# Issuing the weight casts at the start of the program instead of behind the attention strips

## The chip, the cores and the metric

The kernel runs as one program on all 8 NeuronCores of one Trainium2 chip. Each core has its own engines (TensorE, VectorE, ScalarE, GpSimd or POOL, and SyncE, which here only issues DMAs) and 16 DMA engines, and each gets its own copy of the inputs. No core waits for another. The metric is the device time in microseconds (us) of the slowest core.

## The reference

One layer: a layernorm, then an attention-like block with sigmoid scores, a mixture of 8 experts (top 2) plus a shared expert, and the residual. `x` is (2, 8192, 1024).

```python
xn = _layernorm(x, axis=-1)
# attention: C, R = 16, 64; SCALE = 0.03125
qz_u = xn @ ternary_factor_u.T * SCALE          # split into 16 channels of 64
qz_v = xn @ ternary_factor_v.T * SCALE
qh = sigmoid(einsum('bcsr,bctr->bcst', qz_u, qz_v))
qh_v1 = einsum('bcst,bctr->bcsr', qh, qz_v)
qh_v2 = einsum('bcst,bcsr->bctr', qh, qz_u)
message_G = (qh_v1 @ ternary_factor_u + qh_v2 @ ternary_factor_v) * SCALE
# experts: E, H = 8, 2048
w_full = softmax over the top 2 of (xn @ Wr) * SCALE, spread over E
h = einsum('bsd,edh->bseh', xn, W1) * silu(einsum('bsd,edh->bseh', xn, W3))
out = einsum('bsed,bse->bsd', einsum('bseh,ehd->bsed', h, W2), w_full)
out = out + ((xn @ Ws1) * silu(xn @ Ws3)) @ Ws2
return x + message_G + out
```

All inputs are float32. The kernel multiplies in bfloat16.

## The kernel before

A core takes one batch element and owns 2048 of its 8192 rows; it computes `u` and `v` projections for all 8192 rows and everything else for its own. There are four stages.

**Front** (from L383). `ut`, `vt` and `wr` are loaded by 17 DMAs of POOL, which cast float32 to bfloat16 on the way (L393 to L399, semaphore `s_w`); the token of the last is `wprep_tok`. Then 64 tiles of 128 rows are loaded by SyncE (L461, three buffers `xb`), normalized (statistics in `emit_tile_front` at L466 and L469, normalization at L510 in `emit_tile_back`) and transposed (L519). After every fourth tile `emit_group_projs` multiplies the group of 512 rows (L545 feature-major, L573 token-major) and SyncE stores the results to DRAM: `zu_fm` and `zv_fm` (L558), `zu_tm` and `zv_tm` (L587), and for the first four groups `xnT_hb` (L594) beside the router. The loop emits `emit_tile_front(j)` ahead of `emit_tile_back(j - 1)`, so tile 4's load and statistics stand ahead of group 0's projections, and tile 5's load stands behind all stores of group 0 in SyncE's order.

**Strips** (`strip`, L704 to L761). For 16 channels, twice, SyncE loads slices of the stored projections, TensorE computes scores (L724), ScalarE the sigmoid (L750), TensorE the second product (L743). The first waits of this stage are `fence_a = sch.fence()`, which holds the present count of every semaphore.

**Output projection** (L807, L811). 16 DMAs load `ub` and `vb`, the bfloat16 copies of the factors; they wait for `precast_tok`.

**Experts** (`emit_ffn_phase`, L182 to L280). SyncE loads slices of the bfloat16 weights `w1b`, `w3b`, `w2b`, `ws1b`, `ws3b`, `ws2b` from DRAM, which also wait for `precast_tok`; then the residual is added and the result stored.

The bfloat16 copies of the weights are made in DRAM by 29 DMAs of POOL that read float32 and write bfloat16 (L773, L778), 27 of 4 MB written and 2 of 2 MB. Everything is put into per-engine lists by `Sched`; each engine runs its list in order. `Sched.finalize` adds one kind of wait: a DMA that raises a semaphore first waits for the highest count at or below the semaphore's count so far that anyone waits for. So loads and stores of one semaphore are largely issued one behind the landing of another.

Of the kernel before, what the change touches and what calls it, by code (L numbers as in the profile page):

```python
# [20 lines left out]
E = 8  # L21
# [268 lines left out]
def build_nc(debug_stage=4):  # L290
# [5 lines left out]
    u_in = nc.dram_tensor("u_in", [D, D], F32, kind="ExternalInput").ap()  # L296
    v_in = nc.dram_tensor("v_in", [D, D], F32, kind="ExternalInput").ap()
    wr = nc.dram_tensor("wr", [D, E], F32, kind="ExternalInput").ap()
    rb_rep = nc.dram_tensor("rb_rep", [128, E], F32, kind="ExternalInput").ap()
    w1 = nc.dram_tensor("w1", [E, D, H], F32, kind="ExternalInput").ap()  # L300
    w2 = nc.dram_tensor("w2", [E, H, D], F32, kind="ExternalInput").ap()
    w3 = nc.dram_tensor("w3", [E, D, H], F32, kind="ExternalInput").ap()
    ws1 = nc.dram_tensor("ws1", [D, H], F32, kind="ExternalInput").ap()
    ws2 = nc.dram_tensor("ws2", [H, D], F32, kind="ExternalInput").ap()
    ws3 = nc.dram_tensor("ws3", [D, H], F32, kind="ExternalInput").ap()

    out = nc.dram_tensor("out", [OWN, D], F32, kind="ExternalOutput").ap()
# [6 lines left out]
    w1b = nc.dram_tensor("w1b", [E, D, H], BF16, kind="Internal").ap()  # L314
    w2b = nc.dram_tensor("w2b", [E, H, D], BF16, kind="Internal").ap()
    w3b = nc.dram_tensor("w3b", [E, D, H], BF16, kind="Internal").ap()
    ws1b = nc.dram_tensor("ws1b", [D, H], BF16, kind="Internal").ap()
    ws2b = nc.dram_tensor("ws2b", [H, D], BF16, kind="Internal").ap()
    ws3b = nc.dram_tensor("ws3b", [D, H], BF16, kind="Internal").ap()
    ub = nc.dram_tensor("ub", [D, D], BF16, kind="Internal").ap()  # L320
    vb = nc.dram_tensor("vb", [D, D], BF16, kind="Internal").ap()
# [32 lines left out]
    with ExitStack() as ctx:  # L354
# [4 lines left out]
        s_ld = en(nc.semaphore("s_ld"))  # L359
        s_st = en(nc.semaphore("s_st"))  # L360
        s_w = en(nc.semaphore("s_w"))
        sch = Sched([s_t, s_v, s_s, s_ld, s_st, s_w])
# [29 lines left out]
        for dc in range(8):  # L392
            sch.emit("gpsimd", lambda e, dc=dc: e.dma_start(  # L393
                out=ut_sb[:, dc * 1024:(dc + 1) * 1024], in_=ut[dc * 128:(dc + 1) * 128, :]),
                inc=s_w, inc_k=16)
            sch.emit("gpsimd", lambda e, dc=dc: e.dma_start(
                out=vt_sb[:, dc * 1024:(dc + 1) * 1024], in_=vt[dc * 128:(dc + 1) * 128, :]),
                inc=s_w, inc_k=16)
        sch.emit("gpsimd", lambda e: e.dma_start(  # L399
            out=wr_sb, in_=wr.rearrange("(dc p) e -> p dc e", p=128)), inc=s_w, inc_k=16)  # L400
        wprep_tok = sch.tok(s_w)

        if debug_stage == 5:
            sch.emit("sync", lambda e: e.dma_start(
                out=xnT_hb[:, :], in_=tb["xnT_in"][:, :]), inc=s_st, inc_k=16)
            sch.emit("sync", lambda e: e.dma_start(out=wT_sb, in_=tb["wT_in"][:, :]),
                     inc=s_ld, inc_k=16)
# [3 lines left out]
                w1b=w1b, w2b=w2b, w3b=w3b, ws1b=ws1b, ws2b=ws2b, ws3b=ws3b,  # L411
                precast_tok=precast_tok))
            fence = sch.fence()
            sch.emit("sync", lambda e: e.dma_start(out=tb["acc_out"][:, :], in_=acc),
                     waits=fence, inc=s_st, inc_k=16)
# [247 lines left out]
        for j in range(OWN_T):  # L663
            t_tok = sch.emit("tensor", lambda e, j=j: e.transpose(
                a2_ps[0:8, 0:128], wfull_sb[:, j * 8:(j + 1) * 8], idf_sb),
                waits=[wf_tok] + list(tr_free[0]), inc=s_t)
            ev = sch.emit("vector", lambda e, j=j: e.tensor_copy(
                wT_sb[0:8, j * 128:(j + 1) * 128], a2_ps[0:8, 0:128]),
                waits=[t_tok], inc=s_v)
# [96 lines left out]
            strip(zv_fm, zv_tm, zu_fm, qh1_sb)  # L766
            strip(zu_fm, zu_tm, zv_fm, qh2_sb)

        a_done_tok = sch.tok(s_ld)
        first_pc = [True]  # L770
        for ei_ in range(E):
            for (dst_, src_) in ((w1b, w1), (w2b, w2), (w3b, w3)):
                sch.emit("gpsimd", lambda e, dst_=dst_, src_=src_, ei_=ei_: e.dma_start(  # L773
                    out=dst_[ei_], in_=src_[ei_]),
                    waits=([a_done_tok] if first_pc[0] else []), inc=s_w, inc_k=16)
                first_pc[0] = False
        for (dst_, src_) in ((ws1b, ws1), (ws2b, ws2), (ws3b, ws3), (ub, u_in), (vb, v_in)):
            sch.emit("gpsimd", lambda e, dst_=dst_, src_=src_: e.dma_start(  # L778
                out=dst_[:, :], in_=src_[:, :]), inc=s_w, inc_k=16)
        precast_tok = sch.tok(s_w)  # L780


        if debug_stage >= 3:
            fence_s = sch.fence()
            ab.reset_to(32768)
# [2 lines left out]
            for fc in range(8):  # L788
                sch.emit("sync", lambda e, fc=fc: e.dma_start(
                    out=u_sb[:, fc * 1024:(fc + 1) * 1024], in_=ub[fc * 128:(fc + 1) * 128, :]),  # L790
                    waits=fence_s + [precast_tok], inc=s_ld, inc_k=16)
                sch.emit("sync", lambda e, fc=fc: e.dma_start(
                    out=v_sb[:, fc * 1024:(fc + 1) * 1024], in_=vb[fc * 128:(fc + 1) * 128, :]),
                    waits=fence_s + [precast_tok], inc=s_ld, inc_k=16)
# [5 lines left out]
            for dc in range(8):  # L800
                for sg in range(4):
                    pi = gi % 2

                    def do_g(e, dc=dc, sg=sg, pi=pi):
# [13 lines left out]
                        waits=[mm], inc=s_v)  # L818
# [3 lines left out]
        if debug_stage >= 4:  # L822
            emit_ffn_phase(nc, sch, (s_t, s_v, s_s, s_ld, s_st, s_w), ab, af, ps, dict(
                acc=acc, sel_sb=sel_sb, wT_sb=wT_sb, xnT_hb=xnT_hb, const_tok=const_tok,
                w1b=w1b, w2b=w2b, w3b=w3b, ws1b=ws1b, ws2b=ws2b, ws3b=ws3b,
                precast_tok=precast_tok))
# [10 lines left out]
            for j in (range(OWN_T) if RESID else ()):  # L837
                sl = j % 2
                x_tok = sch.emit("sync", lambda e, j=j, sl=sl: e.dma_start(
                    out=xb2[sl], in_=xf[j * 128:(j + 1) * 128, :]),  # L840
                    waits=xb2_free[sl], inc=s_ld, inc_k=16)

                def do_trr(e, j=j):
# [9 lines left out]
                    waits=[tr_tok, x_tok] + ob_free[sl], inc=s_v)  # L853
# [3 lines left out]
                    out=out[j * 128:(j + 1) * 128, :], in_=ob[sl]),  # L857
                    waits=[o_tok], inc=s_st, inc_k=16)
                ob_free[sl] = [st_tok]

        if debug_stage < 4:
            fence = sch.fence()
            pairs = [("zu_fm", zu_fm), ("zv_fm", zv_fm), ("zu_tm", zu_tm), ("xnT", xnT_hb)]
            for (k, src) in pairs:
                sch.emit("sync", lambda e, k=k, src=src: e.dma_start(out=dbg[k][:, :], in_=src[:, :]),
                         waits=fence, inc=s_st, inc_k=16)
            sch.emit("sync", lambda e: e.dma_start(out=dbg["wfull"][:, :], in_=wfull_sb),
                     waits=fence, inc=s_st, inc_k=16)
            if debug_stage >= 2:
                sch.emit("sync", lambda e: e.dma_start(out=dbg["qh1"][:, :], in_=qh1_sb),  # L870
                         waits=fence, inc=s_st, inc_k=16)
                sch.emit("sync", lambda e: e.dma_start(out=dbg["qh2"][:, :], in_=qh2_sb),
                         waits=fence, inc=s_st, inc_k=16)
            if debug_stage >= 3:
                sch.emit("sync", lambda e: e.dma_start(out=dbg["acc"][:, :], in_=acc),
                         waits=fence, inc=s_st, inc_k=16)
# [55 lines left out]
```

How the kernel before makes its waits and increments, by code:

```python
        def op(e, fn=fn, wl=tuple(wl), inc=inc, inc_k=inc_k, prewait=prewait):  # L80
            if prewait[0] is not None:
                e.wait_ge(*prewait[0])
            for (s, v) in wl:
                e.wait_ge(s, v)
            r = fn(e) if fn is not None else None
            if inc is not None and r != "self_inc":
                if r is None:
                    r = e.nop()
                r.then_inc(inc, inc_k)
# [107 lines left out]
                def ld13(e, wsl=wsl, h0=h0, srcs=srcs):  # L197
                    o3 = w13[wsl].rearrange("p (dc x) -> p dc x", dc=8)
                    e.dma_start(out=o3[:, :, 0:256],
                                in_=srcs[0].rearrange("(dc p) h -> p dc h", p=128)[:, :, h0:h0 + 256]).then_inc(s_ld, 16)
                    e.dma_start(out=o3[:, :, 256:512],
                                in_=srcs[1].rearrange("(dc p) h -> p dc h", p=128)[:, :, h0:h0 + 256]).then_inc(s_ld, 16)
                    return "self_inc"
```

## Time and profile before

| what | us |
|---|---|
| median of 2 runs | 11241.76 |
| the two runs | 11203.61, 11279.91 |
| profiled execution, as timed | 11147.0 |
| span of its slowest core (core 7) | 11145.1 |
| spans of its cores | 10733.6 to 11145.1 |

In the profile, L12 is line 12 of the kernel. The engines are PE (TensorE matmuls), PEld (TensorE weight loads), DVE (VectorE), ACT (ScalarE), POOL and SP (SyncE); a `q` behind an engine is its instruction queue, which issues DMAs. L82 and L84 are the waits that `Sched` emits. DMA queue q1 carries what SyncE issues, q0 what POOL issues; a packet in the queue rows is one contiguous piece that one DMA engine moves, or the small write that raises the semaphore at the end. A share is of the 16 DMA engines' time. `arena_b` and `arena_f` are the bfloat16 and float32 buffers in SBUF, and `ps` is PSUM. PEclk is TensorE's granted clock as a share of 2.4 GHz.

### The profile page before, as it was taken

Reading aid. Unit: us, or ns where it says so; the run is one execution under the profiler, and the core shown is the slowest. Engines: PE = TensorE matmul, PEld = TensorE weight load, DVE = VectorE, ACT = ScalarE, POOL = GpSimd, SP = SyncE. Lnnn points to the kernel's source line nnn. Section 1 sums busy time; section 2 is a strip of 40 time slices with the busy share of each in tenths; the row PEclk is TensorE's granted clock in tenths of the full one; section 3 lists DMA queues with packets and bytes.
Section 4 is the critical chain, followed back from the end, with each engine's and each line's share of the span. In section 5 each row is a group of like instructions: output and inputs, shape, how many; then the busy total and the mean of one; then the engine's idle time right before and its main releaser. Section 6 shows DMA issues by size and latency. Waiting matters only on the chain.

```text
span 11145.1 us, 93354 instructions; the slowest of 8 cores (10733.6 to 11145.1 us)
## 1 busy us (share of the span) xinstructions
PE 9510.1 (85%) x35632; PEld 2981.4 (27%) x35632; DVE 1290.9 (12%) x2145; ACT 4734.7 (42%) x4795; POOL 24.5 (0%) x50
## 2 busy tenths in 40 slices
PE   5667789999999999999999996003899999999997
PEld 2233321112222121122221121001344444444443
DVE  3333310000000000000000000000222222222222
ACT  1111137668998795599985696000000010100000
POOL 0000000000000000000000000000000000000000
PEclk8788867669998795599995698556999999999998
DMA  3222210000000000000000039996333333333333
GB/s 82 72 68 72 72 46 17 9 9 18 18 18 18 9 18 14 13 18 18 18 18 9 9 42 110 110 111 81 97 98 89 102 87 98 91 96 97 91 102 117
DMA packets 726796, 635.32 MB, mean 57 GB/s; under 512 B 279256, under 2 KB 611160, under 8 KB 720736
## 3 DMA queue, kind: packets, MB, share of 16 engines
q1 hardware_dynamic: 718976, 507.69, 16.3%
q0 software_dynamic: 7392, 121.65, 9.8%
q8 instruction: 301, 4.93, 0.2%
q14 instruction: 127, 1.04, 0.0%
HBM read 671.24 MB, written 197.13 MB: 78 GB/s over the span
## 4 chain that ended last, share of the span: by engine, by line
PE 54%; ACT 29%; another core or an unknown queue 7%; issue 4%; DVE 3%; DMA 2%; ACTq 0%; SPq 0%; DVEq 0%
ACT arena_b L750 28%; PE ps L213 9%; PE ps L724 9%; PE ps L219 9%; PE ps L743 9%; PE ps L258 7%; PE ps L545 4%; PE ps L573 4%; DMA arena_f<-xf 1%; DVE arena_f L276 1%; DMA arena_b<-w2b 1%; ACT arena_f L466 1%; PE ps L519 1%; PE ps L807 1%
## 5 line engine op out<-in xcount | busy, mean ns | idle before, releaser
L750 ACT ACTIVATE arena_b<-ps 128x1024 bf16<-128x1024 f32 x4096 | 4188.4, 1024 | 1157.5 <-PE ps L743 980.0
L724 PE MATMUL ps<-arena_b 128*64 128x512 bf16 x8192 | 2975.2, 451 | 8.9 <-ACT arena_b L750 6.8
L743 PE MATMUL ps<-arena_b 64*128 64x512 bf16 x8192 | 2891.6, 439 | 38.5 <-ACT arena_b L750 26.7
L228 ACT ACTIVATE arena_b<-ps 128x1024 bf16<-128x1024 f32 x288 | 294.9, 1024 | 2844.2 <-PE ps L219 2844.1
L724 PEld LDWEIGHTS ps<-arena_b 128*64 128x64 bf16 x8192 | 609.9, 115 | 2155.4 <-issue 2150.2
L213 PE MATMUL ps<-arena_b 128*128 128x512 bf16 x4608 | 1080.4, 389 | 48.5 <-DMA arena_b<-w3b 20.6
L258 PE MATMUL ps<-arena_b 128*128 128x512 bf16 x4608 | 1007.3, 381 | 50.7 <-DVE arena_b L231 47.7
L219 PE MATMUL ps<-arena_b 128*128 128x512 bf16 x4608 | 1041.6, 379 | 0.0
L743 PEld LDWEIGHTS ps<-arena_b 64*128 64x128 bf16 x8192 | 471.2, 97 | 2124.2 <-issue 2117.8
L807 PE MATMUL ps<-arena_b 128*128 128x512 bf16 x256 | 62.2, 387 | 830.5 <-DMA arena_b<-vb 830.5
L761 DVE TENSOR_SCALAR arena_b<-ps 128x2048 bf16<-128x2048 f32 x16 | 36.7, 2292 | 5326.1 <-PE ps L724 5326.1
L213 PEld LDWEIGHTS ps<-arena_b 128*128 128x128 bf16 x4608 | 458.5, 100 | 632.0 <-issue 114.7
L258 PEld LDWEIGHTS ps<-arena_b 128*128 128x128 bf16 x4608 | 449.6, 98 | 608.4 <-issue 78.9
L219 PEld LDWEIGHTS ps<-arena_b 128*128 128x128 bf16 x4608 | 450.9, 98 | 543.7
L231 DVE TENSOR_TENSOR arena_b<-ps,arena_b 128x1024 bf16<-128x1024 f32 x288 | 352.6, 1224 | 1745.3 <-ACT arena_b L228 1745.3
L545 PE MATMUL ps<-arena_b 128*128 128x512 bf16 x2048 | 483.3, 401 | 15.2 <-DVE arena_b L526 15.2
L573 PE MATMUL ps<-arena_b 128*128 128x512 bf16 x2048 | 444.6, 379 | 0.0
L519 PE MATMUL ps<-idb_sb,arena_b 128*128 128x128 bf16 x512 | 64.7, 306 | 443.6 <-ACT arena_b L510 217.2
L466 ACT ACTIVATE arena_f<-arena_f 128x1024 f32<-128x1024 f32 x64 | 67.6, 1056 | 830.3 <-DMA arena_f<-xf 753.2
L228 ACT ACT_TABLE_LOAD x1 | 1.3, 1283 | 976.1 <-PE ps L219 976.1
L545 PEld LDWEIGHTS ps<-arena_b 128*128 128x128 bf16 x2048 | 208.2, 102 | 286.6 <-issue 70.8
L573 PEld LDWEIGHTS ps<-arena_b 128*128 128x128 bf16 x2048 | 200.4, 98 | 241.6
(71 smaller groups left out, 1413.7 us busy)
## 6 DMA issues: line engine op xcount, KB each, us to landing
arena_b<-w2b SPq DMA_DIRECT2D x128, 1024.0 KB
arena_b<-w1b SPq DMA_DIRECT2D x128, 512.0 KB
arena_b<-w3b SPq DMA_DIRECT2D x128, 512.0 KB
arena_f<-xf SPq DMA_DIRECT2D x80, 512.0 KB
w1b<-w POOLq DMA_DIRECT2D x8, 4096.0 KB, 435.6
w2b<-w POOLq DMA_DIRECT2D x8, 4096.0 KB, 473.0
w3b<-w POOLq DMA_DIRECT2D x8, 4096.0 KB, 510.4
zu_fm<-arena_b SPq DMA_DIRECT2D x16, 1024.0 KB, 4.6
```

What stands on the lines that cost most here:

```text
L213: e.matmul(ps1[pp][:, hc * 512:(hc + 1) * 512], w13[wsl][:, dc * 512 + hc * 128: dc * 512 + (hc + 1) * 128], xnT_own[:, dc * OWN + sgg * 5 ...
L219: r = e.matmul(ps3[pp][:, hc * 512:(hc + 1) * 512], w13[wsl][:, dc * 512 + 256 + hc * 128: dc * 512 + 256 + (hc + 1) * 128], xnT_own[:, dc ...
L228: si_tok = sch.emit("scalar", lambda e, pp=pp, wsl=wsl: e.activation(sl_sb[wsl], ps3[pp], AF.Silu), waits=[mm_tok] + sl_free[wsl], inc=s_s)
L231: mu_tok = sch.emit("vector", lambda e, pp=pp, wsl=wsl, hgg=hgg, sg=sg: e.tensor_mul(h_sb.rearrange("p (hc s) -> p hc s", hc=16)[:, hgg * ...
L258: r = e.matmul(ps[:, dc * 512:(dc + 1) * 512], w2sl[wsl][:, hc * 1024 + dc * 128: hc * 1024 + (dc + 1) * 128], h_sb[:, (hg * 4 + hc) * 102 ...
L466: sm_tok = sch.emit("scalar", lambda e, sl=sl, c0=c0: e.activation(junk, xb[sl], AF.Identity, accum_out=stats[:, c0:c0 + 1]), waits=[ldt, ...
L519: r = e.transpose(tr_ps[:, dc * 128:(dc + 1) * 128], xn[xsl][:, dc * 128:(dc + 1) * 128], idb_sb)
L545: r = e.matmul(fm_ps[pi][:, 0:512], wsb[:, dc * 1024 + fc * 128: dc * 1024 + (fc + 1) * 128], xnT_stage[st_sl][:, dc * 512:(dc + 1) * 512] ...
L573: r = e.matmul(tm_ps2[tsl][:, fh * 512:(fh + 1) * 512], xnT_stage[st_sl][:, dc * 512 + tt * 128: dc * 512 + (tt + 1) * 128], wsb[:, dc * 1 ...
L724: r = e.matmul(qh_ps[p0:p0 + 64, sgg * 512:(sgg + 1) * 512], tmbuf[sl][:, t * 64:(t + 1) * 64], A_sb2[tp2][b][:, sg * 512:(sg + 1) * 512], ...
L743: r = e.matmul(psc[b][:, sg * 512:(sg + 1) * 512], fmbuf[r0:r0 + 64, t * 128:(t + 1) * 128], ownbuf[r0:r0 + 64, sgg * 512:(sgg + 1) * 512] ...
L750: sig_tok[(t, b)] = sch.emit("scalar", lambda e, b=b, tp2=tp2: e.activation(A_sb2[tp2][b], psc[b], AF.Sigmoid), waits=[sc_tok] + list(last ...
```

## The change

The 29 casts are emitted right behind the 17 preparation loads, at the head of the program, and not behind the strips. The explicit wait for the last load of the strips (`a_done_tok`) goes away. Sizes, order and form of the casts stay, and nothing else changes.

```diff
         sch.emit("gpsimd", lambda e: e.dma_start(
             out=wr_sb, in_=wr.rearrange("(dc p) e -> p dc e", p=128)), inc=s_w, inc_k=16)
         wprep_tok = sch.tok(s_w)
+        first_pc = [False]
+        for ei_ in range(E):
+            for (dst_, src_) in ((w1b, w1), (w2b, w2), (w3b, w3)):
+                sch.emit("gpsimd", lambda e, dst_=dst_, src_=src_, ei_=ei_: e.dma_start(
+                    out=dst_[ei_], in_=src_[ei_]),
+                    inc=s_w, inc_k=16)
+        for (dst_, src_) in ((ws1b, ws1), (ws2b, ws2), (ws3b, ws3), (ub, u_in), (vb, v_in)):
+            sch.emit("gpsimd", lambda e, dst_=dst_, src_=src_: e.dma_start(
+                out=dst_[:, :], in_=src_[:, :]), inc=s_w, inc_k=16)
+        precast_tok = sch.tok(s_w)
@@
             strip(zu_fm, zu_tm, zv_fm, qh2_sb)
 
-        a_done_tok = sch.tok(s_ld)
-        first_pc = [True]
-        for ei_ in range(E):
-            for (dst_, src_) in ((w1b, w1), (w2b, w2), (w3b, w3)):
-                sch.emit("gpsimd", lambda e, dst_=dst_, src_=src_, ei_=ei_: e.dma_start(
-                    out=dst_[ei_], in_=src_[ei_]),
-                    waits=([a_done_tok] if first_pc[0] else []), inc=s_w, inc_k=16)
-                first_pc[0] = False
-        for (dst_, src_) in ((ws1b, ws1), (ws2b, ws2), (ws3b, ws3), (ub, u_in), (vb, v_in)):
-            sch.emit("gpsimd", lambda e, dst_=dst_, src_=src_: e.dma_start(
-                out=dst_[:, :], in_=src_[:, :]), inc=s_w, inc_k=16)
-        precast_tok = sch.tok(s_w)
```

## Rows read from the trace of the kernel before

**Rows 1.** The page: the chain of work that ended last, by engine and by line.
```profile
PE 54%; ACT 29%; another core or an unknown queue 7%; issue 4%; DVE 3%; DMA 2%; ACTq 0%; SPq 0%; DVEq 0%
ACT arena_b L750 28%; PE ps L213 9%; PE ps L724 9%; PE ps L219 9%; PE ps L743 9%; PE ps L258 7%; PE ps L545 4%; PE ps L573 4%; DMA arena_f<-xf 1%; DVE arena_f L276 1%; DMA arena_b<-w2b 1%; ACT arena_f L466 1%; PE ps L519 1%; PE ps L807 1%
```

**Rows 2.** The list of cores: span and mean granted TensorE clock.
```profile
core 3: 11047.0 us, clock 0.841
core 4: 10733.6 us, clock 0.850
```

**Rows 3.** Waits, core 7: us in total, times, longest; TensorE's, then SyncE's.
```profile
PE ps L807 <- DMA arena_b<-vb: 830.5, 1, 830.5
...
SPq L84 <- DMA vb<-v_in: 813.0, 1, 813.0
```

**Rows 4.** Windows, core 7: stretch, busy us of each engine, PEclk, DMA share, GB/s.
```profile
0.00:1500.00 1500.00, 995.76 (x4739) 463.27 (x4739) 479.68 (x1204) 248.85 (x409) 9.70 (x21) 0.83 0.24 73
1512.00:6860.00 5348.00, 5301.50 (x16341) 1078.25 (x16342) 34.37 (x15) 4178.82 (x4087) 14.83 (x29) 0.81 0.12 19
6872.00:7702.00 830.00, 0.19 (x1) 0.00 (x0) 2.29 (x1) 0.00 (x0) 0.00 (x0) 0.50 0.99 114
7702.00:11145.10 3443.10, 3196.18 (x14496) 1435.98 (x14496) 770.76 (x912) 296.20 (x289) 0.00 (x0) 0.96 0.31 94
```

**Rows 5.** Timeline of POOL, first and last of 29 casts; DMA issues: us to landing.
```profile
6625.77 0.54 POOL L773 DMA_DIRECT2D w1b<-w  x1 [6614.72 <-DMA arena_b<-zu_tm]
...
6639.97 0.64 POOL L778 DMA_DIRECT2D vb<-v_in  x1
...
vb<-v_in POOLq DMA_DIRECT2D x1, 2048.0 KB, 1047.7
```

**Rows 6.** Waits of SyncE on cores 3 and 4, then of POOL on core 6.
```profile
SPq L84 <- DMA vb<-v_in: 717.5, 1, 717.5
...
SPq L84 <- DMA vb<-v_in: 385.3, 1, 385.3
...
POOL w1b L773 <- DMA arena_b<-zu_tm: 6609.8, 1, 6609.8
```

**Rows 7.** Timeline of POOL, core 7, and the landing of the same DMA.
```profile
10.01 1.04 POOL L399 DMA_DIRECT2D wr_sb<-wr  x1
...
wr_sb<-wr POOLq DMA_DIRECT2D x1, 16.0 KB, 26.5
```

**Rows 8.** DMA queues, core 7, 6627 to 7690 us: packets, MB, share.
```profile
q0 software_dynamic: 4048, 117.44, 99.5%
```

**Rows 9.** DMA queues, core 7, 15 to 17 us.
```profile
q1 hardware_dynamic: 77, 0.32, 51.2%
q0 software_dynamic: 81, 0.15, 45.6%
```

**Rows 10.** DMA queues, core 2, 6 to 9 us; then core 7, 2 to 3 us.
```profile
q0 software_dynamic: 231, 0.41, 92.4%
q1 hardware_dynamic: 138, 0.00, 5.5%
...
q1 hardware_dynamic: 276, 0.10, 37.1%
```

**Rows 11.** DMA queues, core 7: 69 to 76 us with its store, 97 to 104, 125 to 132.
```profile
q1 hardware_dynamic: 1040, 1.05, 51.3%
...
zu_fm<-arena_b SPq DMA_DIRECT2D x1, 1024.0 KB, 5.6
...
q1 hardware_dynamic: 528, 1.05, 44.1%
...
q1 hardware_dynamic: 153, 0.54, 21.5%
```

**Rows 12.** Timeline and chain, core 7: tile 4's statistics, first store, tile 5's statistics.
```profile
47.26 1.16 ACT arena_f L466 x2
...
70.00 0.38 SPq L558 DMA_DIRECT2D zu_fm<-arena_b  x1
...
131.69 1.06 ACT L466 ACTIVATE arena_f<-arena_f 128x1024 f32<-128x1024 f32 x1 [0.38 <-DVE stats L464]
```

## The prediction

> **What bounds the kernel now.** I read the page first. Its chain of work that ended last gives 7% to "another core or an unknown queue" [rows 1]; one stretch with no compute behind it carries this. The core list shows spans from 10733.6 to 11145.1 us, with core 7 the slowest [rows 2]. The waits of core 7 name the stretch: TensorE stands 830.5 us at L807, the first product of the output projection, and SyncE stands 813.0 us for the landing of `vb` before it may load `ub` and `vb` [rows 3]. The windows cut the program into four: the front (layernorm and projections) to 1500 us with the DMA engines 0.24 busy, the attention strips to about 6860 us, 830 us in which TensorE does nothing and the DMA engines are 0.99 busy, then 3443 us of projection and experts [rows 4]. The casts are issued from 6625.77 to 6639.97 us and the last lands 1047.7 us after its issue, at 7687.7 us [rows 5]. They take 7687.7 - 6625.8 = 1062 us in all, of which about 249 us lie under the last strip and 813 us in the open.
>
> **The 29 casts move: what is removed.** POOL's DMAs are issued behind the 17 preparation loads rather than behind the strips' last load. If they are done by the end of the front, SyncE's wait of 813.0 us goes to nothing. The 17.5 us that TensorE waits beyond it are the fence and the `ub` and `vb` loads, and these stay. On the other cores the wait is shorter: 717.5 us on core 3 and 385.3 us on core 4 [rows 6]. Issuing costs POOL the same 15 us, and nothing is queued behind it.
>
> **When they start and end.** No token between the casts is waited for, but the projections wait for the preparation loads' token, so `finalize` puts a wait for it ahead of the first cast. The last preparation load, `wr`, is issued at 10.01 us and lands 26.5 us later, so the casts start at about 36.5 us [rows 7]. Cores 6 and 7 ran their casts side by side (POOL waited 6609.8 us for its start on core 6, 6614.7 on core 7 [rows 5, 6]), so 1062 us already is a price with the neighbour casting too. I keep it, and no saving for casts that run alone: in the changed kernel all cores begin together. The end is 36.5 + 1062 = 1098.5 us, plus what the front's own packets take from the same engines (below, 15 us): 1113 us.
>
> **What the front gets from the DMA engines meanwhile.** Here is the term that decides. In the stretch of the casts, queue 0 has 4048 packets in 1063 us at a share of 99.5%: 1063 x 0.995 x 16 / 4048 = 4.18 us for one packet, and 4048 / 16 = 253 packets on each engine [rows 8]. How do two queues share an engine? Twice the trace has both at work. From 15 to 17 us they stand 81 to 77 in packets and 45.6% to 51.2% in time, which fits sharing by packets and by bytes alike, since their packets there are alike [rows 9]. On core 2 from 6 to 9 us they are not: queue 1 has packets of 32 bytes (`rb_sb`), and sends 138 in 3 us beside 231 of 2 KB in queue 0, with 5.5% of the time. Alone, core 7's queue 1 sent 276 small packets in 1 us [rows 10]. So a queue gets about one packet per packet of the other, whatever their sizes. I take one for one. The bound below is 138/231 = 0.6 packet per cast packet; above, one queue could hand over several per turn (a rival).
>
> Counted by packets the front is costly. On each engine a store to `zu_fm` or `zv_fm` is 1040/16 = 65 packets, one to `zu_tm` or `zv_tm` 528/16 = 33, a tile load 9 (144 of the 153 packets in its window) [rows 11]; the `xnT_hb` store has the shape of the first kind, 65. Group 0 thus needs 65 + 65 + 33 + 33 + 65 = 261 turns on top of tile 4's load of 9, with 253 turns to be had. At 4.18 us for a cast packet and about 0.07 for ours, a turn is 4.25 us.
>
> **The front's new timetable.** Tile 4 is issued at about 40 us and takes 9 turns, so it lands at 79 us, where ScalarE took it up at 47.26 [rows 12]. ScalarE runs tile 4's statistics ahead of tile 3's normalization, so group 0's projections start 34 us later, and the first store, before at 70.00 us [rows 12], goes out at about 104. SyncE issues in order, each store behind the landing of the one before: 104 + 65 x 4.25 = 380, + 276 = 656, + 33 x 4.25 = 797, + 140 = 937 us for the four. The `xnT_hb` store then gets (1113 - 937)/4.25 = 41 of its 65 turns before the casts end and the rest at once. Our 212 + 41 packets at 0.07 make the 15 us used above. Tile 5's load stands behind that store on the same queue and lands at about 1121 us. Before, ScalarE took it up at 131.69, held by the router and not by the load [rows 12]. From there all runs as before, 1121 - 131.7 = **about 990 us later**. TensorE, VectorE and ScalarE have nothing else to do: group 1 needs tile 5, and the strips need all groups. At 0.6 packet per turn three or four stores of 5.6 us undisturbed [rows 11] are still to come at 1113, so the delay is up to 1010; the term is insensitive on that side.
>
> **What hides nothing more.** The strips' `fence_a` is taken over all semaphores and now holds the casts' count, so the strips can't begin before 1113 us; the front ends at about 1510 + 990 = 2500, so this costs nothing. If the front had kept its pace it would cost nothing either (casts done at about 1400, below). The strips' and the experts' loads meet no casts. In this version 249 us of the casts no longer lie under the last strip, whose TensorE worked on undisturbed: this lost cover is why the sum comes out positive at all.
>
> **The sum.** Core 7: 11145.1 + 990 - 813.0 = 11322 us. Core 3: 11047.0 + 990 - 717.5 = 11320. Core 4: 10733.6 + 990 - 385.3 = 11338, the slowest. Against the profiled execution's 11145.1 that is +193 us. The median shown, 11241.76, lies 97 us above that execution, so I predict 11241.76 + 193 = 11435, rounded to **11430 us** (ratio 1.017).
>
> **The page's rule.** The Trainium skill, "DMA: Bandwidth & Descriptors", section "Queues, rings and completion order", says that each engine goes round-robin between its queue rows but drains a whole packet of about 9 to 17 descriptors before it switches. Read literally, this is the second rival below, and by it the sum would be 11358 us instead of 11430. The rows of core 2 disagree as far as they go: eight 32-byte pieces per engine, drained in one go, would be over in far less than the 3 us seen.
>
> **Rivals.**
> *Bytes are shared, so the front hardly notices* (faster). For it: 0.24 of the DMA engines' time suffices for the front [rows 4], and 1062/(1 - 0.24) = 1397 us of casting fits in 1500. Against it: the 32-byte packets [rows 10]. It would give -813 us, and perhaps twice the chain's 1% for tile loads [rows 1], +220 at most: 11242 - 813 + 110 = 10540 us. Break-even lies where the front gets, during the casts, as far as 1113 - 813 = 300 us of its old time, nearly three groups or some 700 turns of one packet; 2% faster needs 525 us.
> *Several packets of queue 1 per turn.* With 9 cast packets (38 us) against 17 of ours, a store of 65 takes 4 turns, 150 us, one of 33 takes 75 and a load 38. Group 0 is stored by 104 + 150 + 150 + 75 + 75 + 150 = 704, four loads end at 856, group 1's first store runs from 880 to 1030, and at 1113 the front stands where it stood at about 200 us. Delay 913, so 11242 + 913 - 990 + 193 = 11358 us: within 2%.
> *Slower by over 2%.* 11467 us needs 37 us more than forecast. Place and price: the casts themselves. With all four pairs casting beside the front's loads and stores, 4% on 1062 us makes 42. The luck of the strips' clock weighs as much: their granted clock was 0.81 on core 7, and the spans without the wait for `vb` differ (10332 on core 7, 10348 on core 4). The two timed runs are 76 us apart.
> *The casts do not start early.* Only if the wait ahead of the first cast were another than I read: no change, 11242. I give it 1%.
>
> **Chances.** One packet per turn 0.84 (of it 0.58 within 2% and 0.26 above), several per turn 0.07, bytes shared 0.08, no change 0.01. Within 2% (about what a measurement of this kernel can tell from no change) are 0.58 + 0.07 + 0.01 = 0.66; faster 0.08; slower 0.26. The range leaves out the byte rival and some of the upper tail, and takes in several per turn: 11300 to 11530 us.
>
> **What the profile would show.** Right: POOL's cast issues near 37 us; `zu_fm`'s first landing about 275 us after its issue, where it took 5.6; TensorE idle at tile 5's transposes from about 145 to 1120 us; the front's end near 2500; SyncE's wait for `vb` gone, and L807's down to about 17 us. Wrong: first stores landing within some tens of us (bytes shared, or several per turn), casts that take much over 1062 us, or a front that ends before 2000 us.

## The result

The change makes the kernel slower.

| | before | changed |
|---|---|---|
| median, us | 11175.16 (10 runs) | 11437.69 (11 runs) |
| lowest to highest, us | 11048.34 to 11344.01 | 11321.86 to 11702.47 |
| span of the profiled execution, us | 11145.1 | 11321.2 |

The ratio of changed to before is 1.0264, 95% interval 1.0193 to 1.0334; it leaves out the executions in which the cores of one die ran slower than the others, which the table has in it (its medians stand at 1.0235). The kernel is slower beyond doubt, but whether by more than 2% the interval leaves open. The forecast was 11430 us, at a ratio of 1.017 to the median then known.

The page of the changed kernel, core 7, shows in its 40 slices where the time went: TensorE (PE) works a little in the first slice, stands in three, and the DMA engines are full for the first four. The idle stretch that [rows 4] had at 6872 to 7702 us is gone, and a longer one has come at the head.

```profile
PE   2000666779999999999999999999899999999997
...
DMA  9999222220000000000000000000233333333333
```

The windows of core 7 (stretch, busy us of PE, PEld, DVE, ACT, POOL, then PEclk, DMA share, GB/s) put numbers to it. From 100 to 1100 us TensorE is busy for 51 us. The strips and the experts are what they were in [rows 4].

```profile
100.00:1100.00 1000.00, 51.42 (x265) 23.77 (x263) 29.94 (x84) 3.97 (x7) 0.00 (x0) 0.53 1.00 114
2520.00:7850.00 5330.00, 5296.44 (x16339) 1077.65 (x16338) 34.37 (x15) 4177.35 (x4086) 0.00 (x0) 0.82 0.07 14
7860.00:11320.00 3460.00, 3200.89 (x14496) 1438.11 (x14496) 770.92 (x912) 296.21 (x289) 0.00 (x0) 0.96 0.32 95
```

The timelines of core 7 of the changed kernel: POOL's first cast, SyncE's stores and loads of group 0, ScalarE's take-up of tile 5, and the first sigmoid (its table load) of the strips. In the fence after it stands the same first sigmoid of the kernel before.

```profile
37.77 0.54 POOL L405 DMA_DIRECT2D w1b<-w  x1 [26.72 <-DMA wr_sb<-wr]
...
109.62 0.38 SPq L570 DMA_DIRECT2D zu_fm<-arena_b  x1
388.71 0.37 SPq L570 DMA_DIRECT2D zv_fm<-arena_b  x1
672.83 0.36 SPq L599 DMA_DIRECT2D zu_tm<-arena_b  x1
819.95 0.36 SPq L599 DMA_DIRECT2D zv_tm<-arena_b  x1
964.84 0.36 SPq L606 DMA_DIRECT2D xnT_hb<-arena_b  x1
965.36 163.07 SPq L473 DMA_DIRECT2D arena_f<-xf  x4
...
1118.85 1.06 ACT L478 ACTIVATE arena_f<-arena_f 128x1024 f32<-128x1024 f32 x1 [947.92 <-DMA arena_f<-xf]
...
2509.62 1.28 ACT L762 ACT_TABLE_LOAD   x1 [88.17 <-PE ps L755]
```

```profile
1524.32 1.28 ACT L750 ACT_TABLE_LOAD   x1 [87.56 <-PE ps L743]
```

The front ends 2509.6 - 1524.3 = 985 us later. All of it has come by tile 5, which ScalarE takes up at 1118.85 us instead of 131.69 [rows 12], after 947.92 us of waiting for its load. What is won stands in the waits of core 7 before the output projection: "issue" ahead of its first weight load is 17.1 us at the most, where TensorE had stood 830.5 us at this product [rows 3].

```profile
PEld ps L805 <- issue: 18.8, 7, 17.1
```

On core 7 that is +985 - 813 = +172 us, and 11145.1 + 172 = 11317 against a measured span of 11321.2 us.

The DMA queues of core 7 between 110 and 1000 us (packets, MB, share) show what held the front. Both queues have work nearly all the time. They send the same number of packets, 3331 and 3234, and move 97.06 and 4.29 MB.

```profile
q0 software_dynamic: 3331, 97.06, 98.3%
q1 hardware_dynamic: 3234, 4.29, 1.6%
```

Equal counts would also come of turns of several packets each. Windows of about one cast packet's length tell the two apart. From 204 to 209, from 209 to 213.5 and from 213.5 to 218.5 us each queue starts 16 packets each time, as many as there are engines, where turns of several would come in bursts with nothing between them. The first two windows:

```profile
q0 software_dynamic: 16, 0.52, 95.3%
q1 hardware_dynamic: 16, 0.02, 1.2%
...
q0 software_dynamic: 16, 0.52, 103.8%
q1 hardware_dynamic: 16, 0.02, 1.3%
```

### The profile page after: what moved, and what is told of

It is laid out like the page before. It is cut to its first block, busy times and chain, and to the rows that moved or that the text cites. A ratio compares the mean times of both kernels' runs of the same rounds, so it can differ in the third digit from the quotient of the medians.

```text
span 11321.2 us, 93352 instructions; the slowest of 8 cores (11204.5 to 11321.2 us)
## 1 busy us (share of the span) xinstructions
PE 9516.6 (84%) x35632; PEld 2984.3 (26%) x35632; DVE 1291.0 (11%) x2145; ACT 4735.8 (42%) x4795; POOL 24.5 (0%) x50
## 4 chain that ended last, share of the span: by engine, by line
PE 53%; ACT 29%; another core or an unknown queue 8%; issue 3%; DVE 3%; DMA 3%; ACTq 0%; SPq 0%; DVEq 0%
ACT arena_b L762 28%; PE ps L213 9%; PE ps L736 9%; PE ps L219 9%; PE ps L755 9%; PE ps L258 8%; PE ps L557 4%; PE ps L585 4%; DMA arena_f<-xf 2%; DVE arena_f L276 1%; ACT arena_f L478 1%; PE ps L531 1%; PE ps L805 1%; PE ps L809 0%
## 5 line engine op out<-in xcount | busy, mean ns | idle before, releaser
L213 PE MATMUL ps<-arena_b 128*128 128x512 bf16 x4608 | 1075.3, 388 | 47.2 <-DMA arena_b<-w3b 19.3
L258 PE MATMUL ps<-arena_b 128*128 128x512 bf16 x4608 | 1016.6, 383 | 52.0 <-DVE arena_b L231 47.7
L219 PE MATMUL ps<-arena_b 128*128 128x512 bf16 x4608 | 1041.6, 379 | 0.0
L557 PE MATMUL ps<-arena_b 128*128 128x512 bf16 x2048 | 485.4, 403 | 15.2 <-DVE arena_b L538 15.2
L585 PE MATMUL ps<-arena_b 128*128 128x512 bf16 x2048 | 444.6, 379 | 0.0
L531 PEld LDWEIGHTS ps<-idb_sb,arena_b 128*128 128x128 bf16 x512 | 49.6, 138 | 1442.8 <-issue 1442.8
L276 DVE TENSOR_TENSOR arena_f<-ps,arena_f 128x512 f32<-128x512 f32 x256 | 175.2, 685 | 633.0 <-PE ps L258 633.0
```

What stands on the lines that cost most here:

```text
L213: e.matmul(ps1[pp][:, hc * 512:(hc + 1) * 512], w13[wsl][:, dc * 512 + hc * 128: dc * 512 + (hc + 1) * 128], xnT_own[:, dc * OWN + sgg * 5 ...
L219: r = e.matmul(ps3[pp][:, hc * 512:(hc + 1) * 512], w13[wsl][:, dc * 512 + 256 + hc * 128: dc * 512 + 256 + (hc + 1) * 128], xnT_own[:, dc ...
L258: r = e.matmul(ps[:, dc * 512:(dc + 1) * 512], w2sl[wsl][:, hc * 1024 + dc * 128: hc * 1024 + (dc + 1) * 128], h_sb[:, (hg * 4 + hc) * 102 ...
L276: mt = sch.emit("vector", lambda e, dc=dc, sg=sg: e.tensor_mul(t_sb[dc % 2], ps[:, dc * 512:(dc + 1) * 512], wbc[:, sg * 512:(sg + 1) * 512]),
L531: r = e.transpose(tr_ps[:, dc * 128:(dc + 1) * 128], xn[xsl][:, dc * 128:(dc + 1) * 128], idb_sb)
L557: r = e.matmul(fm_ps[pi][:, 0:512], wsb[:, dc * 1024 + fc * 128: dc * 1024 + (fc + 1) * 128], xnT_stage[st_sl][:, dc * 512:(dc + 1) * 512] ...
```

## The experiments

The theory to test: each DMA engine serves the two queues one packet each in turn, so beside casts of 32 KB a packet, the front's small packets get 1.6% of the engines' time. The rival: the casts' bytes, in the DMA engines or in memory, crowd out the front's bytes. Then the size of a packet would not matter, on either side. A second rival: work issued early costs the front its own duration wherever it is put.

### Smaller packets for the casts (e1_early_2k and e2_early_8k)

Both keep the casts at the head of the program and cut each tensor into two column halves, so that the contiguous pieces are 2 KB or 8 KB written. The bytes are the same.

```diff
-                sch.emit("gpsimd", lambda e, ...: e.dma_start(out=dst_[ei_], in_=src_[ei_]), ...)
+        def piece(t, h):                      # CAST_W = 1024 (2 KB) or 4096 (8 KB)
+            k = 2 * CAST_W // t.shape[-1]
+            v = t.rearrange("(a k) d -> a (k d)", k=k) if k > 1 else t
+            return v[:, h * CAST_W:(h + 1) * CAST_W]
+        for (dst_, src_) in pairs_:
+            for h_ in range(2):
+                sch.emit("gpsimd", lambda e, ...: e.dma_start(
+                    out=piece(dst_, h_), in_=piece(src_, h_)), inc=s_w, inc_k=16)
```

> The changed kernel, with each cast cut into two column halves whose contiguous pieces are 2 KB written (4 KB read) instead of 32 KB: same bytes, same early place. Turns by packets: a cast packet then takes about 1062 x 16 / 57344 = 0.30 us, a turn about 0.37 us, so a store to zu_fm lands in about 25 us (279 in the changed kernel), group 0's five stores take under 100 us, and the front loses 0 to 150 us instead of 985: 10340 to 10500 us. Shared bandwidth (bytes): nothing changes but the number of packets, so the front loses the same 985 us or so: about 11320 us. A rival cost: small packets make the casts themselves longer than 1062 us; they may last to the end of the front at 1510 us before that costs anything.

> As the 2 KB version, with pieces of 8 KB written. Turns by packets: a cast packet takes about 1.15 us, a turn 1.22, a store to zu_fm about 80 us, a group of the front about 297 turns or 360 us, so about 3 groups are through when the casts end, where the front stood at about 330 us before: delay about 780 us, 11120 us in all. Shared bandwidth: about 11320 us, as in the changed kernel.

Measured: a profiled span of 11188.4 us with 8 KB (11189.99 us as timed) and of 11119.3 us with 2 KB (11121.04 us as timed; 4 runs, median 11202.18, 11093.84 to 11473.59). On the same chip the kernel before took 11068.93 to 11430.78 us, median 11252.83, so neither version is shown to beat it. The landings of the `zu_fm` and `zv_fm` stores, least, median and largest, are first those of the kernel before, then the changed kernel's, then those with 8 KB and with 2 KB:

```profile
DMA to landing us min/median/max: 4.4/4.5/5.9
...
DMA to landing us min/median/max: 4.4/4.5/283.9
...
DMA to landing us min/median/max: 4.4/4.4/85.9
...
DMA to landing us min/median/max: 4.4/4.7/37.0
```

The slowest store falls with the casts' packets: 284, 86, 37 us at 32, 8 and 2 KB, though the bytes are the same and the engines are as full. This is against the bytes rival and for turns by packets. The delay of the front's end falls too, but less than expected. On core 2 of the 8 KB version the first sigmoid comes at 2377.7 us and on core 3 of the 2 KB version at 2134.6 us, 853 and 610 us late, where I had written 780 and at most 150.

Part of both misses is the casts themselves. The last one lands at 1116.3 us in the changed kernel, at 1189 with 8 KB and at 1308 with 2 KB (`vb`'s second half, issued at 1006.7 and 1005.6, lands 182.7 and 302.2 us later). With 8 KB three groups are through by then, as expected, so the later end explains the 73 us. The expectation for 2 KB had called longer casts harmless up to 1510 us; they are not, since the front runs slowly as long as they last.

The larger part of the 2 KB miss stands in SyncE's timeline (core 3, one group's stores, issued one behind the landing of the other, then the loads, then the next group's first store) and in the queues from 702 to 816 us:

```profile
702.16 0.38 SPq L574 DMA_DIRECT2D zu_fm<-arena_b  x1
735.69 0.38 SPq L574 DMA_DIRECT2D zv_fm<-arena_b  x1
769.26 0.36 SPq L603 DMA_DIRECT2D zu_tm<-arena_b  x1
792.96 0.36 SPq L603 DMA_DIRECT2D zv_tm<-arena_b  x1
815.87 0.36 SPq L610 DMA_DIRECT2D xnT_hb<-arena_b  x1
816.38 64.61 SPq L477 DMA_DIRECT2D arena_f<-xf  x4
918.13 0.38 SPq L574 DMA_DIRECT2D zu_fm<-arena_b  x1
...
q0 software_dynamic: 5403, 10.89, 89.8%
q1 hardware_dynamic: 3136, 4.19, 13.1%
```

A group's five stores take (815.9 - 702.2) + about 32 = 146 us, the last of its four loads is issued by 881 us, and the next group's first store goes out 216 us after this one's, where it took 102 before. I had priced one group's stores and then not carried the sum over the groups that pass during the casts. The turn is dearer as well: a store of 65 packets in 33.4 us is 0.51 us a packet, for a cast packet of 0.30. More than one cast packet goes by per turn: the counts are 3136 to 5403, 0.58 to one, near the 138 to 231 of core 2 in [rows 10]. With 32 KB packets the turns are even.

### Fewer packets for the front (e5_layout_early and its control e6_layout_spread)

The other side of the same ratio: the casts stay as in the changed kernel, and the front's tensors get a layout in which a partition's 8 KB of a store is one run. The strips and the experts read the new layout.

```diff
-                    out=dst[:, g * 512:(g + 1) * 512].rearrange("(fc p) t -> p fc t", p=128),
-                    in_=stg_fm[fsl].rearrange("p (fc t) -> p fc t", fc=8)),
+                    out=dst.rearrange("a b -> (a b)").rearrange("(g p x) -> g p x", p=128, x=4096)[g],
+                    in_=stg_fm[fsl]),
```

The token-major stores and `xnT_hb` are changed likewise. In the control the casts are spread as in e3_spread below.

> The changed kernel (casts early, in pieces of 32 KB), with the intermediate tensors of the front laid out so that a partition's 8 KB of a store is one contiguous run: each of the five stores of a group is then 9 packets on an engine instead of 65 or 33, with the same bytes; the tile loads keep 9. The strips' loads read the new layout in pieces of 1 KB and 128 bytes. Turns by packets: a store lands in about 9 x 4.6 = 41 us (279 in the changed kernel), a group takes 81 turns or 365 us instead of 297 turns, so three groups are through when the casts end and the front loses about 790 us instead of 985: 11125 us. Shared bandwidth or memory: the bytes are the same, so the delay stays 985 and the time 11320 us.

> Control for the layout run: the same layout with the casts spread over the strips (as in e3_spread). Both theories: the layout alone moves the time by less than 30 us, so 10310 to 10370 us (e3_spread's profiled span is 10340).

Measured: 11219.42 us with the early casts (span 11216.6 on core 5, 11064.3 to 11216.6 over the cores). The landings of the feature-major stores and the queues of core 5 from 110 to 1000 us:

```profile
DMA to landing us min/median/max: 3.9/3.9/49.7
...
q0 software_dynamic: 3162, 92.08, 95.0%
q1 hardware_dynamic: 2592, 14.68, 5.1%
```

A store lands in 49.7 us at the most, not 284, with its bytes unchanged, and queue 1 moves 14.68 MB where it moved 4.29, at the same time per packet of the casts. The first sigmoid comes at 2371.5 us on core 5: the front loses 847 us instead of 985. The direction and the landing (41 expected) are those of turns by packets, and "the delay stays 985" is refuted. The delay is 57 us more than expected, and here too the casts last longer: `vb` is issued at 52.5 us and lands 1126.7 us later, at 1179 us, 63 us later than in the changed kernel. By then three groups are through, as expected.

The control took 10581.6 us and so did not stay within 30 us of e3_spread. On its cores 2 to 5 the first sigmoid comes at 1522 to 1525 us, as before, on the other four at 1670 to 1693. Those four ran the front at a lower granted TensorE clock, and so did two cores of the kernel before in another execution, e9_before_again below. The windows from 0 to 1500 us of core 0 and core 2 of the control, then of core 4 of e9_before_again, whose first sigmoid comes at 1695.6 us (third number from the right: PEclk):

```profile
0.00:1500.00 1500.00, 1027.81 (x4283) 448.68 (x4284) 439.32 (x1135) 236.75 (x390) 9.72 (x21) 0.73 0.20 67
...
0.00:1500.00 1500.00, 990.00 (x4653) 464.05 (x4742) 480.95 (x1207) 248.88 (x409) 9.69 (x21) 0.83 0.22 73
...
0.00:1500.00 1500.00, 1025.10 (x4189) 443.52 (x4190) 430.89 (x1123) 236.74 (x390) 9.71 (x21) 0.72 0.22 67
```

The late fronts thus go with the clock and come without the new layout too, while the layout leaves the front at its pace where the clock is 0.83. The experts tell the same: 3307 us on cores at 0.97, up to 3599 on cores at 0.88. In e5 all eight cores reach the first sigmoid between 2366 and 2374 us, so the 138 us it gained belong to the larger packets.

### Casts spread over the strips (e3_spread)

```diff
                     loads = [fm_t, own_t]
+                    emit_cast([tm_t[7]])      # the next of the 29 casts, once this channel is loaded
```

> The kernel before, but one cast is issued in each of the first 29 of the 32 channels of the strips, behind the landing of that channel's loads, so that each of 38 us lies beside loads that are a channel ahead. Both theories: no stall anywhere, the front as before, L807 waits about 17 us instead of 830. From the profiled execution of before that is 11145 - 813 = 10332 us; on median 10360 to 10480. The difference to the changed kernel (median 11438) is then the whole delay of the front, 985 us if the sum is right, and the difference to before is the mean wait of the slowest core, below 813 us where cores cast partly alone.

Measured: median 10374.59 us (5 runs, 10338.86 to 10659.19), where before had 11252.83 (11068.93 to 11430.78) on the same chip. The profiled spans reach 10340.2 us, against 10332 worked out. Waits of core 1:

```profile
PE ps L811 <- DMA arena_b<-vb: 19.5, 1, 19.5
```

This beats both kernels: it keeps the 813 us and does not pay the 985. The changed kernel's profiled execution less this one's is 11321.2 - 10340.2 = 981 us, the front's delay as found in the trace.

### All casts at once, in the strips (e4_strips_all)

```diff
                     loads = [fm_t, own_t]
+                    if c == 1:
+                        emit_cast([tm_t[7]])
+                        while cast_list:
+                            emit_cast()
```

> All 29 casts are issued together once the second channel of the first strip is loaded. Turns by packets: a channel's loads are 530 packets on each engine (512 of 128 bytes), the casts leave 253 turns, so channel 2 or 3 is not loaded before the casts end: TensorE idle about 600 us in the strips, 10930 us in all. Shared bandwidth: the strips use 0.12 of the DMA engines' time, nothing stalls, 10340 us.

Measured: 11027.12 us, near the 10930 of turns by packets and far from 10340. Core 2's waits between 1500 and 2700 us, and its queues from 1600 to 2600:

```profile
PE ps L740 <- DMA arena_b<-zv_tm: 689.1, 3, 256.0
...
q0 software_dynamic: 3700, 107.78, 98.9%
q1 hardware_dynamic: 2927, 1.66, 1.0%
```

The strips ask little of the DMA engines in bytes, 0.12 of their time in [rows 4], and yet TensorE stands 689 us for slices of `zv_tm`. Their packets are 128 bytes, and queue 1 moves 1.66 MB in a millisecond. This is the plainest case against shared bandwidth.

### Early, but paced (e7_paced)

```diff
         def emit_group_projs(g):
             stage_rdy = [tile_info[g * 4 + 3]["ev"]]
+            emit_cast(stage_rdy)              # 16 casts; the other 13 in the first channels
```

> The kernel before with one cast per group of the front, issued when the group's projections may start (16 casts), and the other 13 in the first channels of the strips, one each. Turns by packets: a cast lasts 38 us and gives the front 9 turns, the group's matmuls last 58 us, and its stores have until the next group's loads; the stores that meet a cast land late but the chain has slack, so the front loses 0 to 15 us per group: 10340 to 10580 us. If early casts cost the front their own duration wherever they are put, the loss is 16 x 38 = 600 us: 10940 us.

Measured: 10566.34 us median of 3 (10500.67 to 10710.79), span 10499.1 us on core 5. That core's stores of group 0 and its first sigmoid:

```profile
71.37 0.38 SPq L571 DMA_DIRECT2D zu_fm<-arena_b  x1
99.60 0.37 SPq L571 DMA_DIRECT2D zv_fm<-arena_b  x1
106.17 0.36 SPq L600 DMA_DIRECT2D zu_tm<-arena_b  x1
113.34 0.36 SPq L600 DMA_DIRECT2D zv_tm<-arena_b  x1
117.83 0.36 SPq L607 DMA_DIRECT2D xnT_hb<-arena_b  x1
...
1526.11 1.28 ACT L764 ACT_TABLE_LOAD   x1 [89.96 <-PE ps L757]
```

The first store takes 28 us instead of 5.6, the chain catches up by the fifth, and after 16 casts the front ends at 1526.11 us instead of 1524.32. On cores 2 and 3 it ends some 55 us late, on cores 6 and 7 some 114; their granted clock over the first 1500 us is 0.79 and 0.75, that of the other four 0.82 or 0.83, so this goes with the clock as in e6_layout_spread. A cost of 38 us for each cast wherever it is put would have made 600. It is the queue of casts that costs, not their place.

### Seven early casts (e8_early_seven)

```diff
         wprep_tok = sch.tok(s_w)
+        for _ in range(7):
+            emit_cast()
```

The other 22 go one per channel of the strips.

> The first 7 casts at the head of the program as in the changed kernel, the other 22 one per channel of the strips. Turns by packets: the seven end at 38 + 7 x 37.9 = 303 us with the first store under way; the five stores of group 0 land by about 327, tile 5 at about 333 where it was taken up at 131.7: the front loses 200 us, 10335 + 200 = 10535 us. The delay is then the casts' own duration less 62 us, at 7 casts as at 29.

Measured: median 10641.67 us of 2 runs, profiled span 10543.8 us against 10535 forecast. SyncE on core 2:

```profile
107.03 0.38 SPq L572 DMA_DIRECT2D zu_fm<-arena_b  x1
312.46 0.37 SPq L572 DMA_DIRECT2D zv_fm<-arena_b  x1
317.16 0.36 SPq L601 DMA_DIRECT2D zu_tm<-arena_b  x1
```

The first store lands 205 us after its issue, within 1 us of the last of the seven (issued at 40.13 us, landed 271.5 us later), and the next ones are quick. The front's end is 200 us late on this core (1722.4 us). The queue of casts costs its own duration less 75 us here (275 - 200) and less 93 in the changed kernel (1078 - 985), where I had written 62 for both.

### Both kernels once more (e9_before_again and e10_after_again)

These two are unchanged. They ask how much of the result's 2.6% belongs to the executions.

> The kernel before, profiled once more. The forecast took 813 us as the wait that the slowest core loses, from one execution in which cores 6 and 7 started their casts 5 us apart. If a core's casts run faster while its neighbour is not casting, another execution gives 813 us only where two neighbours of the slowest pair start together, and 400 to 740 us elsewhere (851 to 1062 us of casting), with the slowest core at 11040 to 11150 us. If the casts always take 1062 us, every core waits about 810 us and the fastest and the slowest core differ only by their strips (10900 to 11150 us).

> The changed kernel, profiled once more: all cores cast together from 38 us, so every core's front ends at 2505 to 2520 us and the spans differ by the strips' clock alone: 11100, 11210 or 11320 us, the slowest 11320. If the delay depended on how the cores happen to be aligned, the front's end would vary with the execution.

Measured: the kernel before took 11448.15 us, the changed one 11352.4. SyncE's wait for `vb` in the kernel before is 823.2 and 830.4 us on cores 0 and 1, whose casts start 5 us apart, and 826.7 and 824.8 on cores 6 and 7, 2 us apart. On cores 2 to 5, whose casts start over 100 us apart from their neighbours', it is 715.1, 735.9, 736.0 and 715.5 us:

```profile
SPq L84 <- DMA vb<-v_in: 826.7, 1, 826.7
...
SPq L84 <- DMA vb<-v_in: 715.1, 1, 715.1
```

So a core's casts are faster while its neighbour is not casting, and "always 1062 us" is refuted. My 11040 to 11150 us for the slowest core missed: the experts took about 3590 us on core 6 instead of 3308. Its windows show why:

```profile
8500.00:9000.00 500.00, 469.91 (x2100) 210.64 (x2142) 119.07 (x145) 43.13 (x43) 0.00 (x0) 0.97 0.31 93
9500.00:10000.00 500.00, 480.94 (x1787) 198.59 (x1822) 93.25 (x108) 41.49 (x41) 0.00 (x0) 0.80 0.26 76
```

The clock granted to TensorE falls from 0.97 to 0.80 in the middle of the experts, and 1787 matmuls pass in 500 us where 2100 had. In the changed kernel, the second profile has the first sigmoid of all cores between 2523 and 2537 us, some 20 us later than in the first and outside the 2505 to 2520 expected, and the slowest span is 11350.6 us. Its casts last longer by about as much: `vb` lands 1080 to 1090 us after its issue, in the first profile 1062 to 1071. All cores' casts start together in both, so what another alignment would do to the delay is not shown.

## Why the prediction was right

**Start and end of the casts.** The first cast was to be issued at 36.5 us, behind `wr`'s landing; it was at 37.77. The last piece was to land at 1113 us; `vb` is issued at 51.97 us and lands 1064.3 us later, at 1116.3.

**One packet per turn.** This was the term that decided, taken from 138 and 231 packets on core 2. The changed kernel shows 3331 against 3234, and 16 against 16 in each of three windows of 5 us. The step chosen there, even turns and not 0.6, holds with packets of 32 KB; with 2 KB ones the 0.6 side is the nearer. The only row with unequal packets said 0.6, so that the turns came out even was in part luck, in a term that moves the delay by 20 us at most.

**The timetable.** Issues of the four stores and of `xnT_hb` were worked out as 104, 380, 656, 797 and 937 us, and came at 109.6, 388.7, 672.8, 820.0 and 964.8. Tile 5 was to be there at 1121 and was taken up at 1118.85. The delay of 990 us was 985. A slip in the working is small: the front's packets before `xnT_hb` are 9 + 65 + 65 + 33 + 33 = 205 and not 212, and with the 41 after them they take 17 us at 0.07, not 15.

**What goes away.** L807's wait was to shrink to about 17 us and did. The strips were to wait for no cast, and their 5346 us on core 7 stayed.

**The lost cover.** The 249 us of the casts that lay under the last strip are why the sum came out positive. e3_spread gives all of the casts a cover and gains what was hoped for.

**What was off.** The time was met (11437.69 against 11430), the ratio less well: 1.026 measured, 1.017 forecast, with the interval's lower end at 1.0193. The step is the last of the sum, "the median shown, 11241.76, lies 97 us above that execution". I added +193 us, found from one execution of before, to a median of two runs, and ten runs put that median at 11175.16. The base was thus 67 us too high and the change 70 us too small (193 against 262.5 between the medians), and that the two cancel to 8 us is luck. The term that was probably mis-sized is the wait lost by the slowest core. Its 813 us is the value for two neighbours that start their casts together on the slowest cores. The trace of e9_before_again has 715 to 736 us on four of its cores, and for these the sum is 985 - 725 = +260 us, or 2.3%. The three fastest timed runs of before, 11048 to 11057 us, fit it: 11321.2 - 985 + 715 = 11051, where 813 us of wait gives 11149 and two runs lie at 11146 and 11147. That this pairing is what varied over the timed runs is argued and not shown, since they have no trace; the clock in the experts moves single runs by as much, in either kernel.

The rival with shared bytes is refuted by e4_strips_all and by the packet counts. The rival with several packets per turn is refuted for this pair of queues by the 16 against 16 packets of windows of 5 us, and by the landings: its 704 us for the end of group 0's stores is against 965 for the fourth alone. The upper rival, slower by over 2%, had a chance of 0.26, and the measured ratio lies there while its interval does not exclude less. Its price did not come true: it asked for casts 37 to 42 us longer, and they took 1078 us instead of 1062. The Trainium skill, "DMA: Bandwidth & Descriptors", section "Queues, rings and completion order", has the engines go round-robin between queues, and the trace agrees (3331 packets against 3234). That an engine drains 9 to 17 descriptors before it switches is not what is seen here: each contiguous piece had its own turn, 16 and 16 on 16 engines from 204 to 209 us.

## What to carry to other kernels

Before a bulk transfer is moved beside other DMA work, count packets and not bytes: the other work gets one packet for each packet of the bulk queue (0.58 where those were of 2 KB), so large pieces in bulk starve small ones even where the engines had three quarters of their time to spare. Issue bulk transfers in doses, each behind a token of the work that runs beside it, so that a dose ends before that work's buffers run out (in e3_spread 29 doses, each landed within 45 us of its issue, cost nothing; one queue of 29 cost 985 us). And read such a gain on the slowest core of several executions: a wait that neighbours share is not the same in the next one.

## What the runs showed of the hardware that I had not expected

- With cast packets of 2 KB a small store packet took 0.51 us, more than one cast packet (0.30 us) and itself; with 32 KB packets the turns were even (3331 to 3234). What decides between the two stayed open.
- The granted clock in the experts fell to 0.80 on some cores of some executions (0.81 in each of four windows of 5 us from 9500 us on core 6 of e9_before_again), neither of the levels 1.2 and 2.4 GHz (0.5 and 1.0), and that stage lasted as much as 3676 us instead of 3308. Fronts at a mean of 0.72 or 0.73 instead of 0.83 ended 150 to 175 us later, with 0.81 in the windows of 5 us from 820 to 860 us on core 4 of e9_before_again. The Trainium skill, "TensorE: Matmul & The Clock Gate", Part 1, describes such a state, 13/16 of the clock when three cores of a die run dense matmuls. The value fits. The condition does not: the profiled executions of the kernel before and of the changed one ran all eight cores' experts together at 0.97 or 0.98 (8000 to 10600 and 8000 to 11100 us), and the state came on pairs of neighbours, as on cores 4 and 5 of a front whose cores 6 and 7 kept 0.82 and 0.83.
- The casts ended later where the front moved more bytes beside them: at 1116 us beside 4.3 MB (counted from 110 to 1000 us), at 1179 us beside 14.7 MB in e5_layout_early.
